# Hyperbolic attention: another order of the value products, the q products and the per-batch pieces over the sub-steps of a head

## The reference

```python
alpha = sigmoid(x @ Walpha.T + balpha)                      # one number per row and head
q, k, v = split((x @ Wqkv.T + bqkv))                        # 16 heads of 16
scores_euclid = q k^T / sqrt(D)
qn, kn = (q, k) normalised * safe_scale;  q_hyp, k_hyp = expmap0(qn), expmap0(kn)   # sinh, sqrt
inner = -q_hyp[0] k_hyp[0] + q_hyp[1:] k_hyp[1:]
scores_hyper = -arccosh(max(-inner, 1 + 1e-6))**2 / curv
scores = (1 - alpha) * scores_euclid + alpha * scores_hyper      # causal, 512 x 512 per head
attn = softmax(scores) * spike_mask;  y = attn @ v
x = layernorm(x + y @ Wout.T + bout)
```

## Time and profile before

| | |
|---|---|
| median of 3 runs | 2612.33 us (2603.93 to 2634.62) |
| the profiled execution | 2620.64 us, its span 2618.9 us, mean granted clock 0.804 |
| heads of the first attention | about 109.6 to 1243.4 us of the span, 1133.8 us |

### The profile page before, as it was taken

The page is one execution under the profiler, slowest core; times in us unless marked ns, Lnnn a source line. Parts: engine busy times, 40 slices in busy tenths (PEclk is TensorE's granted clock), DMA queues, the critical chain, the costliest instruction groups (busy, mean ns, idle before and its releaser), DMA issues. The chain is left out here.

```text
span 2618.9 us, 38830 instructions
## 1 busy us (share of the span) xinstructions
PE 2207.4 (84%) x12343; PEld 1169.6 (45%) x12344; DVE 1690.7 (65%) x3493; ACT 1369.2 (52%) x2634; POOL 922.6 (35%) x766
## 2 busy tenths in 40 slices
PE   4589898989999999999468899889888279999991
PEld 2244444444444444444222223223223268888881
DVE  4577878786878778676156655666662545555556
ACT  1366566766666665766225665656656223333332
POOL 4463645554463736433411211221111123333330
PEclk9677687877778786777778988788877689999996
DMA  1210111111121201110141122424524641111116
GB/s 47 66 54 20 57 41 49 49 48 38 37 61 26 62 23 57 33 33 9 39 58 33 26 58 50 113 90 110 133 81 138 261 158 48 47 45 45 48 41 200
DMA packets 140066, 172.35 MB, mean 66 GB/s; under 512 B 23873, under 2 KB 120338, under 8 KB 137874
## 3 DMA queue, kind: packets, MB, share of 16 engines
q1 hardware_dynamic: 131426, 149.58, 20.3%
q0 software_dynamic: 7488, 20.46, 2.6%
q10 hardware_dynamic: 1008, 0.54, 0.1%
HBM read 105.47 MB, written 65.01 MB: 65 GB/s over the span
## 5 line engine op out<-in xcount | busy, mean ns | idle before, releaser
L1243 DVE TENSOR_REDUCE NM<-sP 128x1 f32<-128x512 f32 x512 | 332.6, 684 | 233.4 <-PE sP L1126 231.8
L401 POOL TENSOR_TENSOR YZ<-XL 128x1280 f32<-128x1280 f32 x128 | 297.7, 2326 | 433.2 <-DVE XL L687 400.9
L1058 ACT ACTIVATE PT<-tP 128x512 f32<-128x512 f32 x512 | 285.6, 604 | 260.4 <-PE tP L1138 258.6
L476 ACT ACTIVATE YZ<-YZ,gsc 128x512 f32<-128x512 f32 (+3 forms) x512 | 321.9, 655 | 143.9 <-DVE YZ L663 143.6
L674 DVE CUSTOM_DVE_ANT_0 YZ<-SeP,YZ 128x512 f32<-128x512 f32 (+3 forms) x512 | 244.0, 487 | 228.7 <-PE SeP L541 187.1
L460 ACT ACTIVATE XL<-mP 128x512 f32<-128x512 f32 (+1 forms) x384 | 201.2, 525 | 181.3 <-PE mP L551 180.5
L566 PE MATMUL tPa<-ident,YZ 128*128 128x128 f32 x1280 | 281.4, 346 | 0.3
L1489 ACT ACTIVATE H<-hP,B1T 128x256 f32<-128x256 f32 x312 | 131.0, 471 | 264.5 <-PE hP L1568 264.4
L468 ACT ACTIVATE PTa<-tPa 128x512 f32<-128x512 f32 (+1 forms) x384 | 202.9, 529 | 91.3 <-PE tPa L572 86.9
L540 PE MATMUL SeP<-STG 48*128 48x512 f16 (+3 forms) x512 | 185.0, 361 | 59.4 <-DVE mn L674 58.5
L663 DVE SCALAR_TENSOR_TENSOR YZ<-YZ,XL 128x1280 f32<-128x1280 f32 x128 | 210.5, 1644 | 5.5 <-POOL YZ L401 5.1
(11 more groups left out here) (301 smaller groups left out, 4112.1 us busy)
## 6 DMA issues: line engine op xcount, KB each, us to landing
STG<-planes_a_scratch SPq DMA_DIRECT2D x512, 32.0 KB, 1.9
X<-in_L_ffn_W SPq DMA_DIRECT2D x32, 512.0 KB, 4.2
weight_planes<-X SPq DMA_DIRECT2D x64, 256.0 KB, 2.5
STGb<-planes_scratch SPq DMA_DIRECT2D x96, 128.0 KB, 7.0
planes_a_scratch<-HI SPq DMA_DIRECT2D x64, 128.0 KB, 1.7
planes_a_scratch<-LO SPq DMA_DIRECT2D x64, 128.0 KB, 1.8
STG<-planes_a_scratch SPq DMA_DIRECT2D x128, 64.0 KB, 2.1
Y<-results_scratch SPq DMA_DIRECT2D x16, 512.0 KB, 8.8
```

The lines of the kernel that those rows point to most:

```text
L401: pool.tensor_tensor(YZ[:, h % NYZ, :], XL[:, h % NXL, :], XL[:, h % NXL, :], ALU.mult).then_inc(y_ready, 1)
L476: act.activation(w, w, ACT.Square, bias=gsc[:, b % 2, 1, i, hh:hh + 1], scale=gsc[:, b % 2, 0, i, hh:hh + 1]).then_inc(hyp_ready, 1)
L1058: act.activation(PT[:, p % 4, par, kt, :], tP[x % 3][:, :], ACT.Exp).then_inc(exp_done, 1)
L1243: dve.tensor_reduce(NM[:, g % 2, col:col + 1], sP[n % 2][:, :], AX.X, ALU.max, negate=True).then_inc(max_done, 1)
```

## The change

The table of offsets is written anew, and the value products begin one sub-step earlier with another order of k.

- Value products: k = 0 (512 columns) at 35 = t 3, k = 3 (128) at t 0, k = 2 (256) at t 1, k = 1 (384) at t 2. Each now waits for the part of the exponentials that it reads (AV_NEED) and not for all. ACT's copy of avP moves from t 0 to t 3.
- q pieces: from -66, -63, -60, -57 (three heads) to -65, -61, -57, -53, each at t 3 of a head of its own.
- a from -54 to -51; k from -51, -48 to -49, -47; v from -39, -36 to -45, -37 (v 0 now ahead of the e pieces); e from -45, -42 to -42, -40; h from every third to every second sub-step (-31 to -25); x, y and w by one to two sub-steps.
- DVE's chains move from -51 ... -44 to -48 ... -41, its last step from -35 to -33; POOL's L415 from -48 to -46, its L424 from -39, -37 to -37, -35.

```diff
-            PIECES = [("x", 0, -72), ("x", 1, -69), ("q", 0, -66), ("q", 1, -63), ("q", 2, -60), ("q", 3, -57), ("a", 0, -54),
-                      ("k", 0, -51), ("k", 1, -48), ("e", 0, -45), ("e", 1, -42), ("v", 0, -39), ("v", 1, -36),
-                      ("h", 0, -33), ("h", 1, -30), ("h", 2, -27), ("h", 3, -24), ("y", 0, 107), ("y", 1, 110),
-                      ("w", 0, 113), ("w", 1, 116)]
+            PIECES = [("x", 0, -71), ("x", 1, -69), ("q", 0, -65), ("q", 1, -61), ("q", 2, -57), ("q", 3, -53), ("a", 0, -51),
+                      ("k", 0, -49), ("k", 1, -47), ("v", 0, -45), ("e", 0, -42), ("e", 1, -40), ("v", 1, -37),
+                      ("h", 0, -31), ("h", 1, -29), ("h", 2, -27), ("h", 3, -25), ("y", 0, 105), ("y", 1, 107),
+                      ("w", 0, 111), ("w", 1, 115)]
+            AV_STEPS = [(0, SUB * 8 + 3), (3, SUB * 9), (2, SUB * 9 + 1), (1, SUB * 9 + 2)]
+            AV_NEED = {0: 1, 1: 2, 3: 2, 2: 3}
...
-                        g = at_group(n, SUB * 10)
+                        g = at_group(n, SUB * 9 + 3)
                         if g is not None:
                             act.wait_ge(av_full, g + 1)
...
-                        for k in range(NT):
-                            g = at_group(n, SUB * 9 + k)
+                        for k, offset in AV_STEPS:
+                            g = at_group(n, offset)
...
-                                pe.wait_ge(p_ready, 3 * G * (g + 1))
+                            pe.wait_ge(p_ready, 3 * G * (g + 1) - 3 + AV_NEED[k])
                             for j in range(G):
                                 at = POS[k][0]
                                 mm = pe.matmul(avP[32 * j:32 * (j + 1), k * P:T], VS[:, b % 2, k, G * (g % NG) + j, :],
-                                               PT[:, (G * g + j) % NPT, at:at + T - k * P], start=(k == 0), stop=(k == NT - 1))
-                            if k == NT - 1:
+                                               PT[:, (G * g + j) % NPT, at:at + T - k * P], start=(k == 0), stop=(k == AV_STEPS[-1][0]))
+                            if k == AV_STEPS[-1][0]:
                                 mm.then_inc(av_full, 1)
```

More of the change, by code:

```diff
@@ L407, in _ @@
                                                ALU.mult).then_inc(sq_ready, 1)
-                        b = at_batch(n, -48)
+                        b = at_batch(n, -46)
                         if b is not None:
@@ L418, in _ @@
                         for half in range(2):
-                            b = at_batch(n, -39 + 2 * half)
+                            b = at_batch(n, -37 + 2 * half)
                             if b is not None:
@@ L495, in _ @@
                                 act.activation(QF[:, u % 2, :], mis[:, :], ACT.Copy).then_inc(pb_out, 1)
-                        b = at_batch(n, -52)
+                        b = at_batch(n, -49)
                         if b is not None:
@@ L499, in _ @@
                             act.activation(AI[:, 1, :, :], AI[:, 0, :, :], ACT.Exp, scale=-1.0).then_inc(ea_ready, 1)
-                        b = at_batch(n, -41)
+                        b = at_batch(n, -39)
                         if b is not None:
@@ L736, in _ @@
                             chain(dve.tensor_copy(SQ0[:, 2 * H * i:2 * H * (i + 1)], SQ[:, i, :, 0]))
-                        b = at_batch(n, -51)
+                        b = at_batch(n, -48)
                         if b is not None:
@@ L746, in _ @@
                             chain(dve.tensor_scalar(spk[:, b % 3, :], al[:, :, H], thr[:, 0:1], None, ALU.is_gt))
-                        b = at_batch(n, -50)
+                        b = at_batch(n, -47)
                         if b is not None:
@@ L754, in _ @@
                             chain(dve.tensor_scalar(MK, G1, 1e-8, None, ALU.max))
-                        b = at_batch(n, -48)
+                        b = at_batch(n, -45)
                         if b is not None:
@@ L759, in _ @@
                                 chain(dve.scalar_tensor_tensor(Q, Q, SINH[k], MK, ALU.add, ALU.mult))
-                        b = at_batch(n, -46)
+                        b = at_batch(n, -43)
                         if b is not None:
@@ L766, in _ @@
                             chain(dve.tensor_tensor(A, Q, F2, ALU.mult))
-                        b = at_batch(n, -44)
+                        b = at_batch(n, -41)
                         if b is not None:
@@ L774, in _ @@
                                               rcurv[:, :].unsqueeze(1).broadcast_to([P, NT, H]), ALU.mult).then_inc(stat_ready, 1)
-                        b = at_batch(n, -35)
+                        b = at_batch(n, -33)
                         if b is not None:
```

## The result

The changed kernel takes 2640.1 us (2631.6 to 2656.3, 4 runs) where the kernel before takes 2612.7 on the same footing. The ratio is 1.013, with a 95% interval of 1.008 to 1.018: slower by 1.3%. That is inside the range of 2515 to 2650, near its upper end, but on the other side of the kernel before from the forecast of 2584. A second comparison on another chip gave 1.012 (1.009 to 1.016). Medians are over all executions of a run; the ratios leave out those that fell in a slower state of the chip. The profiled execution took 2656.3 us with a span of 2654.5; it is the slowest of its four, so that its 35.6 us over the span of before overstate the median's loss by some 8 us. Of the 35.6 us, 23.7 lie in the heads, 4.4 before them and 7.5 behind them.

What follows compares the result with a forecast made beforehand. PE looked like the bound, partly through its low clock, with DVE's 115 us the floor of a batch; terms summed to -4.0 us a batch, seven times -28 us, from 2612.3 to 2584 us; range 2515 to 2650.

Steps and rivals of the forecast that it cites:

- Positions 11 to 15 and the a piece: Heads bound by PE, 37.8 us; the a piece leaves them for position 0: -1.9 us a batch.
- Positions 0 to 3, work and the new wait: Heads bound by DVE: added DVE work +2.8 us, DVE's first v write waiting on value products +1.0 us (0 to 4.7).
- Position 4: Longest head, 13.9 us: PE's waits for DVE's v writes go, leaving DVE's work: -2.9 us a batch.
- Positions 5 to 10: 54.5 us: h pieces add 0.7, a clock fall avoided, counted half, saves 3.7: -3.0 us a batch.
- the spared fall: Moving w 0 and the value products might avoid the clock's fall at 625.7 us: 7.3 us less, counted half.
- The value products, costed at nothing: Same columns and count, earlier start: no cost otherwise, under one copy if ACT were late.
- Start and tail: Before and behind the seven batches prepared under heads: a move of under 2 us either way.
- Rival 2: New wait and slow PE in positions 0 to 3, PE's idle time filled: slower, 2643 us; chance 0.22.
- Rival 3: Gains given back through DVE waiting for POOL's square and a clock fall at position 8: 2615 to 2605 us; chance 0.24.
- Rival 1: The clock holds, so positions 5 to 10 lose the low level, 15 us less there: 2507 us; chance 0.12.
- The rule on gaps: Clock loss comes from gaps between matmul bursts, so closing position 4's gaps would suffice; weighed, not counted in the sum.
- section PE-mode transpose: Transposes do not count as busy for the clock in the same way; with that, the trace agreed; no size given.

Runs made afterwards that it cites:

- q3_early: The changed kernel with the last q piece one sub-step earlier (-54 for -53): 2610.7 us, ratio 1.003 to the kernel before.
- v0_late: The changed kernel with v 0 at -38 and v 1 at -35, behind the e pieces: 2666.8 us, ratio 1.022 to the kernel before.
- vh_only: The kernel before with only v 0 at -40 and the h pieces at -31, -29, -27, -25: 2618.0 us, ratio 1.004.
- v0_late_old_av: The changed kernel with v 0 at -38, v 1 at -35 and the value products in their old four steps: 2632.1 us, ratio 1.008.
- qa_old: The changed kernel with the q and a pieces at their old sub-steps, everything else as changed: 2612.1 us, ratio 1.001 to the kernel before.
- after_old_order: The changed kernel with the value products still begun at t 3 but in the old order k = 0, 1, 2, 3: 2630.3 us, ratio 1.009.
- changed_again: The changed kernel unaltered, run again for a comparison on the same chip: 2646.6 us, ratio 1.012 to the kernel before.
- q3_early_v0_late_old_av: The changed kernel with the last q piece at -54, v 0 and v 1 at -38 and -35, value products in old steps: 2608.8 us, ratio 0.999.

## Why the prediction was wrong, point by point

- **Positions 11 to 15 and the a piece.** This is the step that failed. The prediction booked the a piece's leaving as 1.9 us won, "where DVE binds", and the passage of the q piece as 1.9 us of DVE work. It looked up how far v 1 and h 0 stand behind the piece ahead of them, and not a: three sub-steps before, two after, with the readout at t 0 behind DVE's two longest instructions of that sub-step. So it had no term for a wait there. The wait is 2.4 us a batch in PE's own line, in a stretch in which PE feeds DVE. One sub-step more took 1.0 to 1.1% off in each of three pairs of runs, 26 us or 3.8 us a batch. Of that, position 0 has 2.5 to 2.9; the remainder is in the later stretches and the last batch, whose clock fell out differently in the two traces, and is not settled. Where the clock held, positions 11 to 15 were 36.7 to 36.8 us, near the 36 forecast (before: 37.7); in three of five batches of the profiled run it fell there (to 0.96, 0.77 and 0.87), which makes the mean 39.3.
- **Positions 0 to 3, work and the new wait.** Both were sized well: DVE's busy time in the example went from 37.3 to 39.1 us (+1.8, forecast +2.8), and the wait on `av_full` is 1.1 us a batch (forecast 1.0, within 0 to 4.7). (The copy of the q piece was priced at 0.57 us, a mean that holds stretched copies; in the changed kernel 30 of 32 took 0.19. The last section has more of this.) But the stretch grew by 6.7 us, not 3.8, because the sum took it for one that goes by DVE's work alone. DVE's idle time there went from 3.0 to 8.4 us a batch. The wait ahead of a is 2.6 of these 5.4 us, by q3_early, and `av_full` up to 1.1. The rest is open. v 0 in positions 1 and 2 does not explain it: with v 0 in position 3 and no wait on `av_full` (v0_late) the idle time was 8.3 us. The closer k and e pieces and the moved chains of DVE are left, and were not tried by themselves.
- **Position 4.** Larger than forecast, -6.8 for -2.9 us. The term was PE's waits for the v write, and those were worth nothing: vh_only removed them on the kernel before and gained no time. The fault was to count PE's wait where POOL and DVE were as late.
- **Positions 5 to 10.** Forecast -3.0, measured +2.3 in one profiled run of the changed kernel and -0.3 in the other. The low level was there for 28 and 19 us a batch, against 27 before. Two executions of one kernel differ here by nearly as much as the forecast: the term was missed, but by how much is not known. With the old value steps and v 0 late the spared fall did come (v0_late_old_av: 49.3 us, low for 5), in a run that was still 0.8% slower than before.
- **The value products, costed at nothing.** Wrong as a general price: 1.2% on the kernel before and 1.3% under v0_late. Both come with lower clocks of the executions (0.798 and 0.793 as medians, for 0.808 of the kernel before and 0.818 of the run with the old steps); for the second the trace places it in positions 5 to 10. But no loss shows where q and a stand as before: qa_old has the new steps and is at 1.001, and undoing them too (with v 0 late) gave 1.000. How the price hangs on the pieces around was not found, so how much of the changed kernel's 1.3% is theirs stays open; after_old_order puts the order's part at 0.3 to 0.4%.
- **Start and tail.** "Under 2 us either way" was not what the traces showed, +4.4 and +2.8 us ahead of the heads in the two of the changed kernel, but the heads began between 101.7 and 114.5 us in the other kernels, so this can't be told from chance.
- **Rivals.** Rival 2 had the right time (2643 for 2640) and the right stretch, but not its cause: the `av_full` wait was at its low end, the clock in positions 0 to 3 at 0.68 for 0.70, and PE idle for 7.4 of 47.8 us, not filled up. The agreement of the time is luck. Rival 3 has the time of qa_old, 2612 us, but its sign, DVE waiting over 2 us a batch for POOL's square, did not show: 1.8 us in the whole run (6.3 in changed_again). Rival 1 did not happen. The sum of rival 1 also has a slip: the clocks 0.63, 0.95 and 0.65 of the earlier trace rows make 31 us at the low level, not 35, and so 13 us less and not 15, about 2519 us and not 2507.
- **The rule on gaps.** The forecast gave no credit to what the prediction took from the Trainium skill (page TensorE: Matmul & The Clock Gate, section HAM oscillation), and the traces bear that out: 103 us at the low level with PE busy in all of them. What it took from the same page of the Trainium skill on transposes, section PE-mode transpose, is neither shown nor refuted: added products did not raise the clock, but no run here had fewer transposes.

## What to carry to other kernels

In a hand-written pipeline in which pieces share one buffer, write down for each piece which engine reads the one ahead of it, in which sub-step, and behind how much work of that sub-step; a gap of two sub-steps over a heavy one was too short here, and three were enough, for 1% of the run. Ask also which engine stands behind the waiting one: PE's 2.4 us counted because DVE needed what PE had queued behind them. A wait removed from an engine pays only if no other engine is as late at that place: 22 us of PE's waits went here for no gain. The sum of two edits' costs, taken one by one, was not what they did together. And one profiled execution is not its run: the clock differed by enough between two executions of the same kernel to move a batch by 3 us, so read the time and the clock of all executions beside it.

## What was not expected of the hardware

The granted clock stayed at its low level, 1.2 GHz, for 102.9 us while TensorE was busy in all of them, and for 113.7 us with three more 512-column products in each head. Two schedules of the same four value steps (v0_late and v0_late_old_av: another order, a sub-step apart), with the same instructions around them, gave a granted clock of 0.76 or 0.93 in the same stretch of a batch, 57.8 against 49.5 us, and over whole executions 0.791 to 0.795 against 0.815 to 0.826. What decides between them was not found. A higher clock is not a shorter time either: q3_early_v0_late_old_av had 0.818 to 0.833 in its executions and the kernel before 0.805 to 0.823 beside it, and the times are level (0.999).

Not all of DVE's busy time is work. The same instruction, the diagonal (L681, L683 in the changed kernel), took between 0.69 and 2.78 us. In the kernel before 36 of 128 took over one and a half times the shortest, in the changed kernel 60, and the line's sum went from 15.8 to 21.3 us a batch with the same count. The long ones ran beside an instruction of POOL for 78% of their time, the short ones for 7% in the changed kernel; and the 25 long copies of the kernel before (L736, 0.32 to 1.36 us where the other seven took 0.19) all ended within 0.05 us of an instruction of POOL. So it looks as if DVE stands still inside such an instruction while POOL works; no run tested it. It is not what the last q piece changed: q3_early has 60 long diagonals too, and 21.4 us.
